# A four-layer graph network on one core: 11 scatter rounds before the stage change, constants prepared in two parts, the node output bias added to x

## The reference, cut to what matters

```python
hn = relu((x - bn_mean) * rsqrt(bn_var + eps) * bn_weight + bn_bias)
msg = relu(hn[src] + edge_attr) + 1e-7             # 12500 edges
out = softmax_weighted_sum_by_dst(msg) + hn
y = relu(layernorm(out @ W1 + b1) * ln_w + ln_b) @ W2 + b2
x = layernorm(x + (x + y))                         # layer 0: 2x + y
...
h = x @ W_in2f                                     # layer 2
x_ij = h[src] * (ssp(f_ij @ W_f1 + b_f1) @ W_f2 + b_f2) * rcut
y = segment_sum(x_ij, dst)
x = layernorm(x + ssp(y @ W_o1 + b_o1) @ W_o2 + b_o2)
```

## Time and profile before

| what | us |
|---|---|
| median of three runs (2492.06 to 2496.88) | 2494.89 |
| the profiled execution, its own time | 2501.6 |
| its span | 2499.9 |
| setup, until the node stage's first load | 0 to 25.7 |
| node stage `gen_all` | 25.7 to 797 |
| `gin` | 797 to 1125 |
| `edges_first` | 1125 to 1353 |
| `nodes_alone` | 1353 to 1796 |
| `edges_middle` | 1796 to 2158 |
| `edges_last` | 2158 to 2500 |

### The profile page before, as it was taken

One profiled execution on the slowest core, in us unless ns is written; L12 is line 12 of the kernel. 1 busy time (PEld: TensorE's weight loads), 2 busy tenths in 40 slices (PEclk: granted clock), 3 DMA queues, 4 the chain that ended last, 5 costly groups with the idle time before them and its releaser, 6 DMA issues. The chain is left out here.

```text
span 2499.9 us, 45899 instructions
## 1 busy us (share of the span) xinstructions
PE 2119.8 (85%) x14139; PEld 1774.9 (71%) x14139; DVE 1952.0 (78%) x2832; ACT 1792.0 (72%) x3703; POOL 1506.5 (60%) x1114
## 2 busy tenths in 40 slices
PE   4999999999997999998993886888699999476564
PEld 4999999999996777776772775667566666365553
DVE  5999999999995666668992997889688888387464
ACT  4888888888885677776771886778688998365121
POOL 4788766776621444413555656883068885588787
PEclk9999999999998999998996998999899999788676
DMA  3666665555666888867774676887467886676653
GB/s 104 155 156 156 163 161 151 152 160 159 177 171 168 228 253 253 253 208 197 199 172 88 150 179 148 226 231 194 132 171 208 209 212 189 140 165 152 167 163 92
DMA packets 328930, 438.17 MB, mean 175 GB/s; under 512 B 114943, under 2 KB 170593, under 8 KB 328690
## 3 DMA queue, kind: packets, MB, share of 16 engines
q1 hardware_dynamic: 216386, 377.83, 53.1%
q0 software_dynamic: 112000, 56.93, 13.1%
q10 hardware_dynamic: 304, 0.49, 0.1%
HBM read 244.61 MB, written 191.28 MB: 174 GB/s over the span
## 5 line engine op out<-in xcount | busy, mean ns | idle before, releaser
L1730 POOL DMA_INDIRECT acc<-combined,first_ x100 | 206.0, 2060 | 191.7 <-DMA acc<-combined,first_ 96.2
L454 PE MATMUL banks<-mats,g_hT 128*125 128x256 f32 x1000 | 257.6, 380 | 0.0
L474 PE MATMUL banks<-mats,g_zT 128*125 128x128 f32 x2000 | 238.8, 273 | 0.0
L474 PEld LDWEIGHTS banks<-mats,g_zT 128*125 128x125 f32 x2000 | 228.1, 188 | 0.0
L785 POOL DMA_INDIRECT gin_xs<-x,from_ x100 | 127.0, 1270 | 161.0 <-DMA x_of_src<-gin_xs 137.0
L1790 POOL DMA_INDIRECT combined<-h,from_ x100 | 142.8, 1428 | 121.3 <-PE banks L1888 91.4
L454 PEld LDWEIGHTS banks<-mats,g_hT 128*125 128x125 f32 x1000 | 188.4, 188 | 29.6 <-issue 0.2
L518 ACT ACTIVATE g_sq<-banks 125x512 f32<-125x512 f32 x250 | 148.2, 594 | 82.7 <-PE banks L454 82.1
L591 DVE TENSOR_REDUCE g_ss<-g_sq 125x4 f32<-125x1024 f32 x125 | 151.3, 1210 | 63.9 <-ACT g_sq L518 63.9
L535 ACT ACTIVATE g_zT<-banks,cols 128x500 f32<-128x500 f32 x250 | 179.1, 776 | 1.5 <-PE banks L462 1.5
L953 DVE TENSOR_TENSOR gin_acc<-gin_acc,gin_qr 125x512 f32<-125x512 f32 x125 | 86.7, 694 | 116.4 <-ACT gin_qr L915 116.4
(11 more groups left out here) (395 smaller groups left out, 6656.9 us busy)
## 6 DMA issues: line engine op xcount, KB each, us to landing
acc<-g_zero SPq DMA_DIRECT2D x126, 224.0 KB
x<-g_x SPq DMA_DIRECT2D x125, 224.0 KB
g_x<-in_xT SPq DMA_DIRECT2D x100, 250.0 KB
gin_x<-x SPq DMA_DIRECT2D x50, 448.0 KB
h<-gin_hr SPq DMA_DIRECT2D x50, 448.0 KB
al_h<-h SPq DMA_DIRECT2D x40, 448.0 KB
al_x<-x SPq DMA_DIRECT2D x40, 448.0 KB
out<-al_out SPq DMA_DIRECT2D x40, 448.0 KB
```

Source lines behind the costliest of these rows:

```text
L454: m = nc.tensor.matmul(bank[0:P, 256 * j:256 * j + 256], HT[q % 2][:, c:c + P], K.W1c, start=False, stop=j == 1)
L474: m = nc.tensor.matmul(pO[q % 2][0:P, D * j:D * j + D], ZT[q % 2][:, h, P * j:P * j + P], K.W2[:, h, :], start=False, stop=j == R - 1 and ...
L1730: pool.indirect_dma_start(out=K.acc, out_offset=bass.IndirectOffsetOnAxis(ap=K.first[:, g, r:r + 1], axis=0), in_=CR[:, g, r * D:r * D + D ...
```

## The change

- The three later matrix centrings, the centring of the rows of `bo2_rows` and of two of the bias rows, their split, `cm`, `bias_s` and `bias_u` go out of `setup` into a class `Deferred`. VectorE does them inside the node stage, a portion at each of steps 0 to 5, at the head of the step. SP loads their rows there. `bias_s` and `bias_u` are written wide by VectorE, without ScalarE's copies. In `setup` VectorE starts with the two bias rows that remain, before it waits for the matrices.
- ROUNDS is 11 instead of 13.
- The node output bias b2 is no longer a matmul per group. `setup` makes `half` = (b2 less its mean) / 2 as a column with one matmul of `twice` and b2. VectorE adds it to the feature-major x of each node group (`shift`), since x enters the output twice. `hidden` takes the offset `ob` = `o0` - `s0` * `half`, so that its result is as before, and waits for `shift`. For an edge group's target `own` adds `half` as it copies.

```diff
-    K.bias, K.bias_y, K.bias_o = keep("bias", [128, 640], BF16), keep("bias_y", [128, 512], BF16), keep("bias_o", [128, 512], BF16)
+    K.bias, K.bias_y = keep("bias", [128, 384], BF16), keep("bias_y", [128, 512], BF16)
+    K.half, K.ob = keep("half", [128, 1]), keep("ob", [128, 1])
...
-                act.dma_start(rows_[:, :], I["brows"]).then_inc(rows_in, 16)
+                act.dma_start(rows_[:, :], I["brows"][:, 0:384]).then_inc(rows_in, 16)
...
-                for h in range(4):
-                    nc.scalar.activation(K.bias_o[:, 128 * h:128 * h + 128], K.bias[:, 256:384], ACT.Copy).then_inc(wide, 1)
-                for h in range(4):
-                    nc.scalar.activation(K.bias_s[:, 128 * h:128 * h + 128], K.bias[:, 384:512], ACT.Copy).then_inc(wide, 1)
-                    nc.scalar.activation(K.bias_u[:, 128 * h:128 * h + 128], K.bias[:, 512:640], ACT.Copy).then_inc(wide, 1)
-                act.wait_ge(wide, 14)
+                act.wait_ge(wide, 2)
+
+            @block.tensor
+            def _(pe):
+                pe.wait_ge(cols_in, 16)
+                pe.wait_ge(doubled, 1)
+                nc.tensor.matmul(K.ps[0][:, 0:1], K.twice[:, :], K.c("b2o"), start=True, stop=True).then_inc(centred, 1)
...
+                dve.wait_ge(centred, 1)
+                link(nc.vector.tensor_scalar(K.half[:, :], K.ps[0][:, 0:1], 0.25, None, ALU.mult))
+                link(nc.vector.tensor_tensor(K.ob[:, :], K.c("s0"), K.half[:, :], ALU.mult))
+                link(nc.vector.tensor_tensor(K.ob[:, :], K.c("o0"), K.ob[:, :], ALU.subtract))
...
+class Deferred:
+    def load(self, sp):
+        sp.dma_start(self.rows[:, :], self.K.I["brows"][:, 384:640]).then_inc(self.rows_in, 16)
...
+    def on_vector(self, dve, n):
+        nc, K, rows, rest, part = self.nc, self.K, self.rows, self.rest, self.part
+        if n == 0:
+            self.centre(dve, K.W("o2"))
+            self.centre(dve, K.W("W2lT"))
+        elif n == 1:
+            self.centre(dve, K.W("W2rT"))
+            self.centre(dve, K.bo2_rows)
+        elif n == 2:
+            dve.wait_ge(self.rows_in, 16)
+            self.centre(dve, rows[:, 0:D])
+            self.centre(dve, rows[:, D:2 * D])
+            self.link(dve, nc.vector.tensor_scalar(K.cm[:, :], K.ident[:, :], 1.0, -1.0 / 128, ALU.mult, ALU.add))
+        elif n == 3:
...
+        elif n in (4, 5):
...
+            self.link(dve, nc.vector.tensor_scalar(wide, part[0], K.ident[:, 0:1], None, ALU.mult))
+            for i in (1, 2):
+                self.link(dve, nc.vector.scalar_tensor_tensor(out=wide, in0=part[i], scalar=K.ident[:, i:i + 1], in1=wide,
+                                                              op0=ALU.mult, op1=ALU.add))
...
                 load(0, 0)
                 load(1, 1)
+                df.load(sp)
...
                 def second(q):
                     past(pe, x1, q - 2)
-                    nc.tensor.matmul(pO[q % 2][0:P, :], K.ones_all[:, 0:P], K.bias_o[:, :], start=True, stop=False)
-                    for j in range(R):
-                        nc.tensor.matmul(pO[q % 2][0:P, D * j:D * j + D], X[q % NX][:, P * j:P * j + P], K.twice[:, :], start=False, stop=False)
+                    for j in range(R):
+                        nc.tensor.matmul(pO[q % 2][0:P, D * j:D * j + D], X[q % NX][:, P * j:P * j + P], K.twice[:, :], start=j == 0, stop=False)
...
                 def hidden(q):
...
-                        act.wait_ge(x_in[q % NX], landed[q])
+                        past(act, shifted, t)
...
-                    nc.scalar.activation(HT[q % 2][:, :], X[q % NX][:, :], ACT.Relu, bias=K.c("o0"), scale=K.c("s0")).then_inc(hid, 1)
+                    nc.scalar.activation(HT[q % 2][:, :], X[q % NX][:, :], ACT.Relu, bias=K.ob[:, :], scale=K.c("s0")).then_inc(hid, 1)
...
-                    nc.scalar.activation(X[q % NX][:, :], pE[:, 0:G], ACT.Copy).then_inc(xdc, 1)
+                    nc.scalar.activation(X[q % NX][:, :], pE[:, 0:G], ACT.Identity, bias=K.half[:, :]).then_inc(xdc, 1)
...
+                def shift(q, t):
+                    dve.wait_ge(x_in[q % NX], landed[q])
+                    nc.vector.tensor_scalar(X[q % NX][:, :], X[q % NX][:, :], K.half[:, :], None, ALU.add).then_inc(shifted, 1)
...
-                walk(seq, [(-5, "edge", maximum), (1, "all", reduce), (-4, "edge", fall), (4, "all", reduce_o), (-1, "edge", share),
+                walk(seq, [(0, "all", lambda q: df.on_vector(dve, q)), (-5, "edge", maximum), (1, "all", reduce), (-4, "edge", fall), (4, "all", reduce_o), (-1, "edge", share),
...
-                           (-1, "edge", join), (4, "all", apply), (-7, "edge", positive), (-8, "edge", runs_of), (-5, "edge", falls),
+                           (-1, "edge", join), (-3, "node", shift), (4, "all", apply), (-7, "edge", positive), (-8, "edge", runs_of), (-5, "edge", falls),
...
-        ROUNDS, PAIRS = 13, NG // 2 - LATE
+        ROUNDS, PAIRS = 11, NG // 2 - LATE
```

More of the change, by code:

```diff
@@ L25 @@
         ("beta", "L1_gnn_beta"), ("bf1", "L2_gnn_b_f1"), ("bf2", "L2_gnn_b_f2"), ("bo1", "L2_gnn_b_o1"),
-        ("b1l", "L3_gnn_b1l"), ("b2l", "L3_gnn_b2l"), ("t", None)]
+        ("b1l", "L3_gnn_b1l"), ("b2l", "L3_gnn_b2l"), ("b2o", "L0_gnn_b2"), ("t", None)]
 COLS = [n for n, _ in VECS] + ["s0", "o0", "tmp"]
@@ L157, in tmp @@
             return ctx.enter_context(nc.sbuf_tensor(name, shape, dt))
-        rows_ = tmp("brows", [128, 640])
-        part = [tmp(f"bpart{i}", [128, 640], BF16) for i in range(3)]
-        rest = [tmp(f"brest{i}", [128, 640]) for i in range(2)]
+        rows_ = tmp("brows", [128, 384])
+        part = [tmp(f"bpart{i}", [128, 384], BF16) for i in range(3)]
+        rest = [tmp(f"brest{i}", [128, 384]) for i in range(2)]
         mean, mean2 = tmp("mean_w", [128, 2]), tmp("mean_w2", [128, 4])
         fl, fl2 = tmp("fl", [P, EG, R]), tmp("fl2", [P, EG, R])
+        doubled, centred = sem("doubled"), sem("centred")
         cols_in, mats_in, rows_in, idx_in, f1_in = sem("cols_in"), sem("mats_in"), sem("rows_in"), sem("idx_in"), sem("f1_in")
@@ L218, in _ @@
                 link(nc.vector.memset(K.ones3[:, :], 1.0))
-                dve.wait_ge(mats_in, 16)
-                link(nc.vector.reduce_sum(mean[:, 0:1], K.W1c, AX.X))
-                link(nc.vector.tensor_scalar(mean[:, 1:2], mean[:, 0:1], 1.0 / 256, None, ALU.mult))
-                link(nc.vector.tensor_scalar(K.W1c, K.W1c, mean[:, 1:2], None, ALU.subtract))
-                link(nc.vector.reduce_sum(mean2[:, 0:2], K.W2, AX.X))
-                link(nc.vector.tensor_scalar(mean2[:, 2:4], mean2[:, 0:2], 1.0 / 128, None, ALU.mult))
-                for h in range(2):
-                    link(nc.vector.tensor_scalar(K.W2[:, h, :], K.W2[:, h, :], mean2[:, 2 + h:3 + h], None, ALU.subtract))
-                dve.wait_ge(rows_in, 16)
[L228 to L235, removed]
+                dve.wait_ge(rows_in, 16)
+                for a, b in ((0, 256), (256, 384)):
                     link(nc.vector.reduce_sum(mean[:, 0:1], rows_[:, a:b], AX.X))
@@ L245, in _ @@
                 dve.wait_ge(consts, 3)
-                link(nc.vector.tensor_scalar(K.twice[:, :], K.ident[:, :], 2.0, -2.0 / 128, ALU.mult, ALU.add))
-                link(nc.vector.tensor_scalar(K.cm[:, :], K.ident[:, :], 1.0, -1.0 / 128, ALU.mult, ALU.add))
                 link(nc.vector.tensor_scalar(K.bias[:, :], part[0][:, :], K.ident[:, 0:1], None, ALU.mult))
@@ L252, in _ @@
                 nc.vector.memset(mean[:, 0:1], 0.0).then_inc(split, 1)
+                dve.wait_ge(split, 1)
+                link(nc.vector.tensor_scalar(K.twice[:, :], K.ident[:, :], 2.0, -2.0 / 128, ALU.mult, ALU.add))
+                nc.vector.memset(mean2[:, 0:1], 0.0).then_inc(doubled, 1)
+                dve.wait_ge(doubled, 1)
+                dve.wait_ge(mats_in, 16)
+                link(nc.vector.reduce_sum(mean[:, 0:1], K.W1c, AX.X))
+                link(nc.vector.tensor_scalar(mean[:, 1:2], mean[:, 0:1], 1.0 / 256, None, ALU.mult))
+                link(nc.vector.tensor_scalar(K.W1c, K.W1c, mean[:, 1:2], None, ALU.subtract))
+                link(nc.vector.reduce_sum(mean2[:, 0:2], K.W2, AX.X))
+                link(nc.vector.tensor_scalar(mean2[:, 2:4], mean2[:, 0:2], 1.0 / 128, None, ALU.mult))
+                for h in range(2):
+                    link(nc.vector.tensor_scalar(K.W2[:, h, :], K.W2[:, h, :], mean2[:, 2 + h:3 + h], None, ALU.subtract))
                 dve.wait_ge(sq, 2)
@@ L320, in walk, with __init__, link, centre @@
                     stage(q, seq[q][1])
+class Deferred:
+    def __init__(self, nc, K, ctx):
+        self.nc, self.K, self.count = nc, K, 0
+        self.made, self.rows_in = K.sem("df_made"), K.sem("df_rows")
+        self.rows, self.rest = [ctx.enter_context(nc.sbuf_tensor(f"df_{n}", [128, 2 * D], F32)) for n in ("rows", "rest")]
+        self.part = [ctx.enter_context(nc.sbuf_tensor(f"df_part{i}", [128, 2 * D], BF16)) for i in range(3)]
```

(28 more changed lines are left out.)

## The result

| | before | after |
|---|---|---|
| median, six runs each, taken together | 2495.89 (2485.58 to 2504.23) | 2470.05 (2465.95 to 2474.95) |
| profiled execution, its span | 2499.9 | 2467.7 |

The ratio is 0.9893, 95% interval 0.9872 to 0.9913: the change saves 27 us (22 to 32). The forecast was 2488.4, so three quarters of the gain were not in its sum. The first rival, that TensorE's relief counts, was priced at 2472.

A forecast was written before the change was run, and what follows sets the result against it. TensorE was taken to bound the node stage, with VectorE 8% short of being next; -9.5 + 0 + 3 + 0 = -6.5 us took the profiled 2501.6 to 2495.1, so the median to 2488.4, range 2478 to 2497.

The forecast's parts named there:

- The first rival: Node stage: TensorE's relief counts, 14 steps take 82.5 us or so, -16 in the dense part, 2472 in all; chance 0.18.
- Setup, -9.5: Preparation before the node stage: ends at 15.2 instead of 24.78 us, -9.5 us (-10.3 to -7.7).
- TensorE's loss, 27 us at most: Node stage: 125 bias matmuls of 0.22 us each leave TensorE, 27 us, the most this part can give.
- Dense part, 0: Node stage after its first steps: VectorE passes TensorE, 84.4 us per 14 steps, 0 us (-14 to +24).
- VectorE's work: Node stage, VectorE's start-to-start slots per 14 steps: 77.2 us before, 82.7 after with 11 shifts of 0.5.
- The collision with POOL: Node stage: one in three shifts long beside POOL's DMA instructions; if most are, a slower rival, 2512, chance 0.15.
- The idle time: Node stage: 1.7 us per 14 steps that VectorE cannot use, between light and heavy steps.
- the slot of 0.5: Node stage: mean VectorE time per shift near 0.5 us, 0.4 undisturbed and 0.76 at worst.
- First steps, +3: Start of the node stage: deferred constants in six portions and the first shift delay VectorE, +3 us (+1 to +5).
- Eleven rounds, 0: First edge pipeline ends about 25.5 us earlier, but the alone-nodes stage stops longer for POOL's gathers: 0 us (-4 to +6).
- The second rival: Alone-nodes stage: the nodes' stop is not tied to POOL, 14 rounds end about 25 us sooner, 2463; chance 0.07.
- The signs: Expected in the profile: TensorE no longer full in the node stage, VectorE at 97% or more, 84 us per 14 steps.

The follow-up runs named there:

- the third session: The changed kernel, unaltered, measured again beside three other kernels on one chip: ratio 0.9904 (0.9873 to 0.9935) against the kernel before.

## Why the prediction was wrong, point by point

**Setup, -9.5: right.** -10.1, inside the bounds. VectorE starts on the bias rows at 3.59, not 4.5.

**TensorE's loss, 27 us at most: right.** Putting a matmul back cost 24.8.

**Dense part, 0: wrong; this is the step that failed.** 84.4 us per 14 steps were predicted, 82.0 came: -20.8 over 8.3 cycles. Three sizes made up the error, all in VectorE's account.
- *VectorE's work.* 77.2 + 11 x 0.5 = 82.7. Measured from 60 to 740, VectorE is busy for 670.82 of 680 us, 80.9 in each 82.0; before it was 623.88, 77.5 in each 84.5. The rise is 3.4, not 5.5. Cheaper `positive` operations explain 3 x 0.12 of the gap, so a shift takes 0.34 (3.8 / 11), while its record shows 0.475: records overlap their neighbours' by more than I took off.
- *The collision with POOL.* One in three `positive` records was long before, and I carried that share over to the shifts. Of 90 shifts one was long (0.70 us), though 75 began under a POOL DMA instruction. Before, 8 of 25 `positive` records were long, of 21 that began under such an instruction. What decided was how far that instruction had come: the 8 long ones began 0.81 to 0.91 us into it, the 13 short ones within the first 0.53. After, all 15 `positive` records that began under one did so 1.03 us into it or later, and none was long. The shifts began within the first 0.38 us or from 1.05 us on, but for two, at 0.74 (the long one) and at 1.00.
- *The idle time.* I charged 1.7 us per 14 steps that VectorE could not use. It was 1.1 (82.0 - 80.9).

The long shift, and a short `positive` of the kernel after, each behind its POOL instruction:

```profile
64.35 1.19 POOL L445 DMA_INDIRECT row_of<-d_slot,to_d  x1 [0.30 <-issue]
65.08 0.70 DVE L668 TENSOR_SCALAR g_x<-g_x,half 128x500 f32<-128x500 f32 x1
...
271.46 1.32 POOL L433 DMA_INDIRECT g_xs<-in_x,idx  x1 [0.31 <-issue]
272.61 0.41 DVE L690 TENSOR_SCALAR g_ms<-g_ms 128x500 f32<-128x500 f32 x1
```

The other runs agree. Over all 14 profiles kept here, from 60 to 740 us, 97 of 1314 shifts and `positive` records are longer than 0.6 us. Every one of them began 0.52 to 0.99 us into a POOL DMA instruction and ended 0.22 to 0.25 us after it; of the 859 that began in its first 0.51 or its last 0.24 us, none took over 0.5. So a share of long records goes with the place in the step, and can't be carried from one operation to another.

With 80.9 of work TensorE's 81.4 stays the larger, and the stage comes within 0.6 us of it. The rival put this at 82.5 and the whole at 2472. Its argument, that VectorE had already reached 96% in heavy stretches without holding TensorE up, was the better reading, and it had a chance of 0.18. The end of my range for this term, -14 "if VectorE is never idle", was too narrow also, since it kept the slot of 0.5.

By the Trainium skill, page SBUF — State Buffer, section SBUF: two separate sides, the port pair that VectorE and GpSimd share is an exclusive lock, kept for the whole instruction, where VectorE's operation is in a mode of two ports; no run shows the mode. For POOL's DMA instructions the trace does not agree with the whole instruction: 74 of 75 shifts that began under one ran at their short duration, and the long records all began in its later middle. By the Trainium skill, page Perfetto Trace Analysis, section Identifying the Most-Contended Engine, one goes for the engine of highest occupancy, and judges TensorE by its weight loads. That was TensorE, with 186.41 of 200 us of weight loads beside VectorE's 183.26; the trace agrees, and gave 18 to 21 of the 27 us.

**First steps, +3: low.** -15.9 + 20.8 leaves +4.9; read directly, the first `twice` matmul stands 21.7 us behind the stage's start, and 17.6 before. The late portions were in the sum. Two things weren't. One is the load: "a shift waits for its group's load ... : 0". On ScalarE that wait stood ahead of `hidden` of the same group alone; on VectorE it is three steps ahead of its use, with the first reduction behind it (2.64 us of waiting in the kernel after, 4.48 in the third session). The first reduction starts 1.7 us after the square that it needs (26.48 and 24.22 + 0.60). The other is TensorE's clock:

```profile
25.00:28.00 3.00, 0.81 (x4) 0.35 (x2) 2.49 (x7) 0.27 (x1) 2.39 (x3) 1.00 1.03 295
28.00:31.00 3.00, 1.95 (x5) 1.57 (x6) 2.63 (x6) 1.41 (x4) 2.39 (x3) 0.60 0.37 67
```

TensorE waits 3.23 us for the first `scale`, and the granted clock goes to its lower level (0.60 in the mean from 28 to 31 us, 0.83 from 31 to 34; 1.00 in the kernel before from 25 to 46). One half of `first` and the transposes behind it take 3.4 us from 29.05, and 2.0 at the full clock from 35.29: 1.4 us lost. Without shifts the clock stays at 1.00 and the start is 4.7 us earlier; how that divides between the wait, the shift and the clock, no run shows.

**Eleven rounds, 0: right.** -3.9 for the two stages together, and 0.9998 for the edit by itself. By mechanism too: SP's stop grew from 14.4 to 33.4 us. The rounds beside the nodes came 14.2 apart, not 14.9: 199.0 us from round 11 to the first gather, for fourteen. The second rival (the nodes aren't tied to POOL) fell.

```profile
1300.26 1.98 POOL L1789 DMA_INDIRECT acc<-combined,first_  x1 [9.79 <-POOLq L113]
...
1499.26 1.26 POOL L1804 DMA_INDIRECT combined<-acc,from_  x1 [3.21 <-DMA acc<-combined,first_]
```

**The signs.** TensorE was named as no longer full and VectorE as at 97% or more. VectorE was (99%), TensorE stayed at 99.9%, and the list had called that a proof of error: it was. The next load after the first gather was to be issued 6 us earlier: it was 34 us earlier (1548.05 to 1514.09), of which 27.0 are the earlier start of the first edge pipeline. The alone stage began 53.5 us earlier (1353.0 to 1299.5) and not 32, for the same reason: both follow from the node stage.

**What stays open.** The worth of the divided preparation is 4 us by the profiles; the two pairs of times give 12 us (0.9950 and 0.9904) and -2 us (0.9905 and 0.9914), too far apart to say more. `positive` ran long where it began in the later middle of a POOL DMA instruction (8 of 23 again, 542 ns in the mean, when the matmul is put back); what sets the place at which it begins wasn't tried, nor what POOL does there.

## What to carry to other kernels

When work moves from a full engine to one at 92%, add it up in start-to-start distances and busy time, not in record durations: there were 1.8 us of 82.7 between "becomes the bound" and "hidden". An engine that saves time ahead of an in-order queue saves nothing until that queue's first wait on another engine is late enough; look for the entry that stops the queue, move it by what the stop lasts plus some steps to spare, and move it again when the work it waits for grows. An operation moved to another queue takes its wait with it: ask what stands behind it there. And the price of a collision with another engine's instruction goes by where in it the operation begins, so read it at the operation's own place in the step.

## What had not been expected

- Two engines at 99% side by side: TensorE 199.73 and VectorE 197.83 of 200 us, in a pipeline whose steps differ (5.6 to 6.1 us).
- SP's order of its queue held back some 50 us: moving the copies five steps and more later gave nearly twice what the whole change did.
- A POOL DMA instruction under way lengthened 1 of 75 shifts, but 8 of 21 `positive` operations of the same shape, and in all 14 profiles it did so only where they began 0.52 to 0.99 us into it.
- The chips of two sessions differ by 2% on one kernel (2544.8 and 2495.9 us); the node stage of the kernel after took 780.8 and 756.0.
